# Four graph layers on one core: the features enter in rows, three split steps are kept from pass 3 to pass 4, and the timetables of the layer norm work change

## What is computed

```
x = ln(x + L0(x));  L0: h = relu(adj @ (f1 * (adj @ (x @ W1)))),  out = adj @ (f2 * (adj @ (h @ W2)))
x = ln(x + L1(x));  L1: concat(x, adj @ x) @ Wcat
x = ln(x + L2(x));  L2: m = x @ W_msg + b;  g = sigmoid((m@W_q)(m@W_k).T / sqrt(128) + bias) * adj * adj
                        r = relu(concat(x, g @ m) @ W_upd + b_upd);  out = ln(r) * gamma + beta
x = ln(x + L3(x));  L3: twice: x = swish((adj @ x) @ W3 + b3)
```

## Time and profile before

| | us |
|---|---|
| median of 3 runs | 1653.19 (1652.88 to 1653.26) |
| the profiled execution | 1654.23 |
| its span | 1652.4 |

### The profile page before, as it was taken

The page is one execution under the profiler, slowest core; times in us unless marked ns, Lnnn a source line. Parts: engine busy times, 40 slices in busy tenths (PEclk is TensorE's granted clock), DMA queues, the critical chain, the costliest instruction groups (busy, mean ns, idle before and its releaser), DMA issues.

```text
span 1652.4 us, 19276 instructions
## 1 busy us (share of the span) xinstructions
PE 1605.6 (97%) x7674; PEld 766.8 (46%) x7674; DVE 1212.3 (73%) x1181; ACT 1099.3 (67%) x784; POOL 56.0 (3%) x49
## 2 busy tenths in 40 slices
PE   7999999999999999999999899999999999999997
PEld 4444444444444444444554444444354444444443
DVE  5867547754675568666998698998989986553886
ACT  5767648756778567855666587796878685453753
POOL 2000000000000000000000000100000100000011
PEclk9999999999999999999999999999999999999999
DMA  9988798979699889986888345554545898764983
GB/s 360 416 315 354 283 427 337 369 284 427 269 417 427 333 314 372 411 321 263 355 309 305 140 180 180 178 209 172 199 163 199 312 375 303 282 235 173 351 295 118
DMA packets 67562, 484.56 MB, mean 293 GB/s; under 512 B 7712, under 2 KB 7872, under 8 KB 9232
## 3 DMA queue, kind: packets, MB, share of 16 engines
q1 hardware_dynamic: 66240, 478.70, 75.2%
q0 software_dynamic: 1088, 4.56, 0.8%
q10 hardware_dynamic: 144, 0.07, 0.0%
HBM read 414.09 MB, written 69.21 MB: 292 GB/s over the span
## 4 chain that ended last, share of the span: by engine, by line
PE 81%; DVE 10%; issue 5%; ACT 3%; DMA 1%; POOL 0%; SPq 0%; DVEq 0%; POOLq 0%; ACTq 0%
PE acc L594 34%; PE acc L606 17%; PE spare L594 12%; PE spare L606 6%; PE spare L629 4%; PE rows L498 3%; DVE a_lo L998 3%; DVE a_lo L989 3%; PE acc L629 2%; PE rows L491 1%; DVE bn L905 1%; ACT a_hi L792 1%; DMA a_ring<-adj_dram 1%; DVE gates L1011 1%; ACT gates L822 1%
## 5 line engine op out<-in xcount | busy, mean ns | idle before, releaser
L989 DVE SCALAR_TENSOR_TENSOR a_lo<-a_ring,a_hi 128x2048 f16<-128x2048 f32 x320 | 723.9, 2287 | 321.9 <-ACT a_hi L792 316.5
L792 ACT ACTIVATE a_hi<-a_ring 128x2048 f16<-128x2048 f32 x320 | 604.9, 1905 | 286.7 <-PE spare L594 156.1
L594 PE MATMUL acc<-a_hi,y_hi 128*128 128x512 f16 x1536 | 459.9, 380 | 4.2 <-ACT a_hi L792 3.5
L594 PE MATMUL acc<-a_hi,y_lo 128*128 128x512 f16 x1536 | 459.5, 380 | 0.0
L606 PE MATMUL acc<-a_lo,y_hi 128*128 128x512 f16 x1536 | 406.2, 380 | 9.1 <-DVE a_lo L998 4.9
L606 PEld LDWEIGHTS acc<-a_lo,y_hi 128*128 128x128 f16 x1536 | 149.7, 98 | 193.5 <-DVE a_lo L998 8.1
L594 PEld LDWEIGHTS acc<-a_hi,y_lo 128*128 128x128 f16 x1536 | 150.7, 98 | 182.3 <-issue 2.2
L594 PEld LDWEIGHTS acc<-a_hi,y_hi 128*128 128x128 f16 x1536 | 150.5, 98 | 182.0 <-issue 6.0
L1011 DVE SCALAR_TENSOR_TENSOR gates<-gates,a_ring 128x1024 f32<-128x1024 f32 x128 | 155.8, 1218 | 35.8 <-ACT gates L822 35.6
L805 ACT ACTIVATE a_hi<-gates 128x1024 f16<-128x1024 f32 x128 | 134.8, 1053 | 41.2 <-DVE gates L1011 41.0
L998 DVE TENSOR_TENSOR a_lo<-gates,a_hi 128x1024 f16<-128x1024 f32 x128 | 155.5, 1215 | 0.0
(11 more groups left out here) (119 smaller groups left out, 760.9 us busy)
## 6 DMA issues: line engine op xcount, KB each, us to landing
a_ring<-adj_dram SPq DMA_DIRECT2D x326, 1024.0 KB, 7.4
saved_squares<-squares SPq DMA_DIRECT2D x64, 1024.0 KB, 12.6
a_ring<-saved_squares SPq DMA_DIRECT2D x64, 1024.0 KB, 4.8
x_T<-xt_dram SPq DMA_DIRECT2D x4, 512.0 KB, 8.6
x_rows<-x_dram POOLq DMA_DIRECT2D x1, 2048.0 KB, 12.9
out_dram<-x_rows POOLq DMA_DIRECT2D x3, 512.0 KB, 2.9
out_dram<-x_rows SPq DMA_DIRECT2D x2, 256.0 KB, 2.0
w<-W_dram POOLq DMA_DIRECT2D x2, 64.0 KB, 5.4
```

Source lines behind the costliest of these rows:

```text
L594: mm = pe.matmul(sums[:, h * BANK:(h + 1) * BANK], blk(y[:, y_pass % 2, :], st.j0 + s), slot(a_hi, st)[:, s, h * BANK:(h + 1) * BANK], sta ...
L792: act.activation(slot(a_hi, st), loaded(st), ACT.Copy, scale=2.0 ** A_EXP).then_inc(s_ahi, 1)
L989: dve.scalar_tensor_tensor(out=slot(a_lo, st).rearrange("p s c -> p (s c)"), in0=loaded(st).rearrange("p s c -> p (s c)"), scalar=2.0 ** A ...
```

## The change

- Pass 0 has no projection any more. SP loads `x` in rows in the place of the transposed input, ACT and DVE split it as it is, and the epilogue of pass 1 multiplies by W1 where it transposed (adj @ (x @ W1) = (adj @ x) @ W1). POOL's load of `x` goes.
- `KEPT` has an entry for pass 3: three steps of its first block stay for pass 4, in the room of `x_T`, and of `xn` and `tmp`. `lead` and `halves_free` follow.
- The squares of (0,2) move from pass 2 to pass 4, those of (1,1) from 4 to 2.
- The fifth pass's last chunk, whose epilogue lies in the gated pass, gets a table of its own (`LAST_FIFTH`): evacuation at 1, statistics in two pieces at 4 and 5, normalising at 7, and the rest up to 17.
- In the gated pass the first layer norm is applied by ACT in four pieces of two blocks (`normalise_first`, `xn` = the normalised value), gamma and the residual are two half-size operations each on DVE, statistics come in pieces, the second normalising is four pieces at 26 to 29, y_high is at 30 and y_low at 31 (both at 23 before). The last chunk's table moves one stage later.
- ACT makes one sigmoid of a single column after y_high of chunk 2 of pass 5, which puts the load of the sigmoid's table there.
- In the tail the second half's moments come ahead of the first half's normalising.

```diff
-SAVED_IN = {(2, 0): 1, (3, 0): 1, (3, 1): 1, (2, 3): 2, (1, 3): 2, (0, 3): 2, (0, 2): 2, (1, 0): 3, (2, 1): 3,
-            (3, 2): 3, (1, 2): 4, (0, 1): 4, (3, 3): 3, (2, 2): 3, (1, 1): 4, (0, 0): 4}
+SAVED_IN = {(2, 0): 1, (3, 0): 1, (3, 1): 1, (2, 3): 2, (1, 3): 2, (0, 3): 2, (0, 2): 4, (1, 0): 3, (2, 1): 3,
+            (3, 2): 3, (1, 2): 4, (0, 1): 4, (3, 3): 3, (2, 2): 3, (1, 1): 2, (0, 0): 4}
...
-KEPT = [(i, (j * GROUP + t) * SJ) for i, j, t in ((0, 0, 3), (0, 3, 0), (0, 2, 2), (0, 2, 3), (1, 3, 1), (1, 3, 2))]
+def kept_steps(*steps):
+    return [(i, (j * GROUP + t) * SJ) for i, j, t in steps]
+
+
+IN_SQUARES, IN_X_T, IN_ROWS = RING, RING + SQUARE_SLOTS, RING + SQUARE_SLOTS + 2
+KEPT = {3: dict(zip(kept_steps((1, 1, 1), (1, 1, 2), (1, 1, 3)), (IN_X_T + 1, IN_ROWS, IN_X_T))),
+        7: dict(zip(kept_steps((0, 0, 3), (0, 3, 0), (0, 2, 2), (0, 2, 3), (1, 3, 1), (1, 3, 2)),
+                    (IN_SQUARES, IN_SQUARES + 1, IN_SQUARES + 2, IN_SQUARES + 3, IN_X_T, IN_X_T + 1)))}
...
+SECOND_USES = [n for n, u in enumerate(UNITS) if u.p != u.step.p]
...
-LENGTH = {0: 1, 1: 4, 2: 3, 3: 4, 4: 8, 5: 11, 6: 23, 7: 4, 8: 10, LAST_GATED: 14}
+LAST_GATED, LAST_FIFTH = 10 + GATED, 15
+LENGTH = {0: 1, 1: 4, 2: 3, 3: 4, 4: 8, 5: 11, 6: 32, 7: 4, 8: 10, LAST_GATED: 15, LAST_FIFTH: 17}
 
 
 def timing(p, k):
 
-    return LAST_GATED if (p, k) == (GATED, NC - 1) else p
+    return {(GATED, NC - 1): LAST_GATED, (5, NC - 1): LAST_FIFTH}.get((p, k), p)
...
         def lead(st):
 
             n = LAST_IN_PASS[st.n - RING] + 1 if st.n >= RING else 0
-            return max(n, FIRST_USE[st.n] - RING) if st.p == PASSES else n
+            return max(n, FIRST_USE[st.n] - RING) if any(n <= u < FIRST_USE[st.n] for u in SECOND_USES) else n
 
         def halves_free(eng, st, used):
 
             n = SLOT[st.n]
             if HALVES_BEFORE[st.n] is not None:
                 eng.wait_ge(used, freed(st))
-            elif n >= RING + SQUARE_SLOTS:
+            elif n >= IN_ROWS:
+                eng.wait_ge(s_wqk_product, 1)
+                eng.wait_ge(s_bias, 2 * BIAS_STEPS)
+            elif n >= IN_X_T and st.p > GATED:
                 eng.wait_ge(s_rows, nth("rows", GATED, NC - 1))
-            elif n >= RING:
+            elif IN_SQUARES <= n < IN_X_T and st.p > GATED:
                 eng.wait_ge(s_lg, NB * NC)
+            elif IN_SQUARES <= n < IN_X_T:
+                for t in range(SQUARE_SLOTS):
+                    eng.wait_ge(s_stored[t], 16 * len(SQUARED) // SQUARE_SLOTS)
...
-            if n < RING + SQUARE_SLOTS:
-                v = squares[:, n - RING, :].bitcast(F16)
+            if n < IN_X_T:
+                c = n - IN_SQUARES
+                pair = squares[:, 0:SJ, :] if t is a_hi else squares[:, SJ:2 * SJ, :]
+                return pair.bitcast(F16)[:, :, c * CH:(c + 1) * CH]
+            if n == IN_ROWS:
+                v, at = (xn_T if t is a_hi else tmp_T).bitcast(F16), 0
             else:
-                v = x_T[:, (n - RING - SQUARE_SLOTS) * SJ * CH:(n - RING - SQUARE_SLOTS + 1) * SJ * CH].bitcast(F16)
-            at = 0 if t is a_hi else SJ * CH
+                v = x_T[:, (n - IN_X_T) * SJ * CH:(n - IN_X_T + 1) * SJ * CH].bitcast(F16)
+                at = 0 if t is a_hi else SJ * CH
...
-                sp.dma_start(x_T[:, ic * CH:(ic + 1) * CH], xt[:, ic * CH:(ic + 1) * CH]).then_inc(s_xt[ic], 16)
+                sp.dma_start(x_chunk(0, ic), x[:, ic * CB:(ic + 1) * CB, :]).then_inc(s_x[ic], 16)
...
-                if p in (1, 3, 4):
+                if p in (3, 4):
                     transposes(lambda b: blk(z_T, b))
                 elif p == 5:
                     by_node((x_T_chunk(p, k), wcat[:, 0, :]), (z_T, wcat[:, 1, :]))
                 elif p == 6:
                     bias(bupd_rows)
                     by_node((x_T_chunk(p, k), wupd[:, 0, :]), (z_T, wupd[:, 1, :]), begins=False)
-                elif p == 0:
-                    by_node((x_T_chunk(p, k), w1[:, :]))
+                elif p == 1:
+                    by_node((z_T, w1[:, :]))
...
-                0: {0: [project]},
...
-                LAST_GATED: {1: [project]},
+                LAST_GATED: {2: [project]},
+                LAST_FIFTH: {2: [project], 9: [x_transposes], 11: [messages], 13: [queries], 16: [message_rows]},
...
+                if p == 0:
+                    act.wait_ge(s_x[k], 16)
...
+            def sigmoid_table(p, k):
+
+                if k == 2:
+                    act.activation(stats[:, 2, 0:1], gbias[:, 0:1], ACT.Sigmoid)
...
+            def normalise_first(blocks):
+                def go(p, k):
+                    act.wait_ge(s_shift, 2 * k + 1)
+                    for b in blocks:
+                        op = act.activation(xn[:, b, :], val[:, b, :], ACT.Identity, bias=stats[:, 2, b:b + 1],
+                                            scale=stats[:, 1, b:b + 1])
+                    if blocks[-1] % HB == HB - 1:
+                        op.then_inc(s_first, 1)
+                return go
...
-                    9: [qk_high(1, qT_hi, Q_EXP)], 10: [y_high]},
-                6: {1: [evacuate], 5: [relu], 20: [normalise_again(range(HB))], 21: [normalise_again(range(HB, CB))],
-                    23: [y_high]},
+                    9: [qk_high(1, qT_hi, Q_EXP)], 10: [y_high, sigmoid_table]},
+                6: {1: [evacuate], 5: [relu], 13: [normalise_first([0, 1])], 14: [normalise_first([2, 3])],
+                    15: [normalise_first([4, 5])], 16: [normalise_first([6, 7])], 26: [normalise_again([0, 1])],
+                    27: [normalise_again([2, 3])], 28: [normalise_again([4, 5])], 29: [normalise_again([6, 7])],
+                    30: [y_high]},
                 7: {0: [evacuate], 2: [silu], 3: [y_high]},
                 8: {0: [evacuate], 3: [silu]},
-                LAST_GATED: {0: [evacuate], 3: [relu], 11: [normalise_again(range(CB))], 14: [y_high]},
+                LAST_GATED: {0: [evacuate], 4: [relu], 12: [normalise_again(range(CB))], 15: [y_high]},
+                LAST_FIFTH: {1: [evacuate], 10: [save_x_T], 12: [save_m_T], 13: [qk_high(0, kT_hi, K_EXP)],
+                    14: [qk_high(1, qT_hi, Q_EXP)], 17: [y_high]},
...
+            def some_stats(ready, stage, blocks):
+                def go(p, k):
+                    dve.wait_ge(ready, nth(stage, p, k))
+                    block_stats(blocks)
+                return go
+
+            def all_stats(run):
+                def go(p, k):
+                    join_stats(range(CB), CB * (nth("root", p, k, run) - 1))
+                return go
+
+            def gamma_half(h):
+                def go(p, k):
+                    dve.wait_ge(s_first, HALVES * k + h + 1)
+                    dve.tensor_tensor(half(xn, h), half(xn, h), gam[:, :].unsqueeze(1).to_broadcast([P, HB, F]),
+                                      ALU.mult).then_inc(s_scaled, 1)
+                return go
+
+            def residual_half(h):
...
+                    dve.wait_ge(s_xb, k + 1)
+                    dve.wait_ge(s_scaled, HALVES * k + h + 1)
+                    op = dve.tensor_tensor(half(val, h), half(xn, h), half(x_chunk(p, k), h), ALU.add)
+                    if h == HALVES - 1:
+                        op.then_inc(s_res, 1)
+                return go
...
-                6: {8: [ln_moments(0, s_nl, "nonlin")], 10: [times_gamma], 13: [affine_residual],
-                    16: [ln_moments(1, s_res, "resid")], 19: [shift], 23: [y_low]},
+                6: {6: [some_stats(s_nl, "nonlin", [0, 1])], 7: [some_stats(s_nl, "nonlin", [2, 3])],
+                    8: [some_stats(s_nl, "nonlin", [4, 5])], 9: [some_stats(s_nl, "nonlin", [6, 7]), all_stats(0)],
+                    11: [shift(0)], 16: [gamma_half(0)], 17: [residual_half(0)], 18: [gamma_half(1)],
+                    19: [residual_half(1)], 20: [some_stats(s_res, "resid", [0, 1, 2, 3])],
+                    21: [some_stats(s_res, "resid", [4, 5, 6, 7])], 22: [all_stats(1)], 24: [shift(1)], 31: [y_low]},
                 7: {3: [y_low]},
                 8: {0: [take_over], 5: [residual], 6: [ln_moments(0, s_res, "resid")], 7: [normalise]},
-                LAST_GATED: {4: [ln_moments(0, s_nl, "nonlin")], 5: [times_gamma], 6: [affine_residual],
-                    8: [ln_moments(1, s_res, "resid")], 10: [shift], 14: [y_low]},
+                LAST_GATED: {5: [ln_moments(0, s_nl, "nonlin")], 6: [times_gamma], 7: [affine_residual],
+                    9: [ln_moments(1, s_res, "resid")], 11: [shift(1)], 15: [y_low]},
+                LAST_FIFTH: {3: [values], 4: [some_stats(s_val, "val", [0, 1, 2, 3])],
+                    5: [some_stats(s_val, "val", [4, 5, 6, 7]), all_stats(0)], 7: [normalise],
+                    14: [qk_low(0, kT_hi, kT_lo, K_EXP)], 15: [qk_low(1, qT_hi, qT_lo, Q_EXP)], 17: [y_low, add_beta]},
...
             moments_half(0)
+            moments_half(1)
             normalise_half(0)
-            moments_half(1)
             normalise_half(1)
...
```

(14 more changed lines are left out.)

57 lines of the change are left out of this document (28 added, 29 removed).

## The result

The changed kernel takes 1641.16 us (median of 4 runs, 1640.63 to 1642.51) against 1653.22 (1652.88 to 1655.44) for the kernel before on the same chip: ratio 0.9925, 95% interval 0.9911 to 0.994. That is 12.1 us less, where 16.5 was forecast. It is faster, by 0.7%, and inside the range of 1628 to 1645. It is outside the 1632.5 to 1640.5 that the forecast called its own, by 0.7 us, and close to the 1641.5 to 1641.9 of the rivals (b), (c) and (e).

The account below looks back on a forecast made before the run. PE's pace, 2.59 us per step of 12 products, bounds the kernel outside waits, start and tail; -8.8 + 3.4 - 1.9 + 0.8 - 5.9 - 9.1 + 6.1 - 1.1 = -16.5 us gives 1636.7, range 1628 to 1645.

Parts of the forecast that it names:

- (b): At the start: the DMA holds it, 4.8 us less gained, time 1641.5; chance 0.12.
- (c): Gated chunks: waits stay in another form, gain only 1.3 us per chunk, 3.9 in all, time 1641.9; chance 0.12.
- (e): Start and pass 7: three more half-clock stretches of 3.4 us, +5.1, time 1641.8; chance 0.06.
- Part 5: Entry to pass 7: longer chain to y_low +4.4, half clock behind PE's wait +1.7, together +6.1 us (0 to +7).
- Part 2: Steps kept from pass 3 to 4: -1.9 us (0 to -2.5); squares moved to pass 2: +0.8 (0 to +3).
- Part 4: Gated chunks: waits go, -11.7 us; ACT's pieces cost +2.6 at two chunk ends; together -9.1 (-5 to -11.7).
- The start's 1.2 for a DMA without lead: First ten steps: 1.2 us taken off the 10.0 gain, as PE needs 405 GB/s against the DMA's 421.
- (a): Pass 7 doesn't begin later, as ACT and DVE leave the gated pass further ahead: 6.1 less, 1630.6; chance 0.14.
- (d): Gated pass: ACT becomes the bound through its pieces, gated chunks +14.4 us, time 1660.2; chance 0.04.

Follow-up runs that it names:

- The old pieces: The changed kernel with the epilogue of the gated pass's first three chunks as before the change (24 stages, statistics in one piece): 1646.91 us, 5.8 more.

## Why the prediction was right, and where its sizes were off

Sign, order of size and the named places held, but for the chunks, 89.05 us apart where 87 to 89 was named. The gain was 12.1 of a forecast 16.5, and outside the forecast's own range. The parts, from the first product's start of the same unit in the two profiles:

| part | forecast | profiles | undone or done alone |
|---|---|---|---|
| x in rows, W1 in pass 1 | -5.4 | -4.7 | -3.1 alone |
| kept steps; squares moved | -1.9; +0.8 | -2.2; +0.8 | -2.8 (kept) |
| pass 5, units 284 to 300 | none | +0.7 | in four of 13 profiles |
| entry to the gated pass, from unit 300 | -5.9 | -6.3 | -4.8 |
| gated chunks | -9.1 | -8.1 | -5.8 |
| entry to pass 7 | +6.1 | +7.1 | +2.8 |
| tail | -1.1 | -0.8 | -2.4, with a half clock |
| half clock in pass 4 | none | +1.7 | in one of this kernel's two profiles |
| sum | -16.5 | -11.8 | |

**Right as worked out.** The tenth step at 38.95 for 39.2, because DVE is last: from 22.75 on its a_lo and y_lo follow one another without a pause, 2.2 and 1.1 us each. The squares cost 0.8 and no more. The entry to the gated pass lost both waits and the half clock, 6.3 us in ten of the eleven profiles that have the new table, and 6.4 in the one without the early load. The entry to pass 7 took 4.4 us more before its clock is counted, the very sum of one a_lo 2.2, y_lo 1.2 and ACT 1.0. (The stretch of the earlier trace rows is not quite "without a pause": DVE waits 2.85 us for a_hi at 1326.83 before, and as long at 1313.13 after, so the difference stands.) The old pieces bear this split out: there the 2.2 of y_lo and ACT are absent, and from the gated pass's end to block (0,3) that kernel loses 2.2 where the changed one loses 4.4.

**The step that failed: the clock.** Part 5 spoke of "less left half clock behind it" and priced it at 1.7 us, one stretch of 3.4 as in the earlier trace rows. It was 6.8 us long in both profiles of the changed kernel, and in three of the six others with the same wait of 4.6; it was 3.4 in the other three. 1.3 us of it lay in the wait itself, the other 5.5 cost half, 2.7. Nothing at all was set down for pass 4, where the a_lo wait of 2.1 had run at full clock in the profile before. Part 2 said that the later waits of passes 4 and 5 have nothing changed ahead of them, and that is so for the waits. What follows a wait is another matter. Together these are 2.7 of the 4.7 us that the profiles fall short.

**The other mis-sized terms.** Part 4 gave 1.3 us to a chunk's end, 4 x 0.25 + 0.3; the 89.05 less PE's own 86.9 and the 0.4 leaves 1.8. The cost per step with pieces was even smaller than put (2.72 less 2.59, 0.13 against 0.25, which was 0.3 a few lines earlier), but ACT does not come to them on time: it starts 1.1 late, since its a_hi wait for DVE's gates, and with nothing to absorb it in the single buffer, the whole 1.7 is PE's. The start's 1.2 for a DMA without lead was 1.7 in the first profile, and from 1.1 to 3.0 over all of them. The tail's DVE work ends 1.1 sooner behind the last product, as forecast (7.1 against 8.2), but only 0.8 reaches the end of the span. The 0.7 in pass 5 was not foreseen: the chain to DVE's normalise of chunk 0 begins there at a load that landed at 790.35, while in a profile without the loss PE is not held by a load.

**The rivals.** (a) and (d) are excluded: pass 7 does begin later, and ACT is no bound. (b) is partly alive: the start's lead varies by 1.9 us between profiles, and the part alone gave 3.1. (c) fell: the old waits went, 8.1 us in the profiles. By the time alone (b), at 1641.5, came closest, but the start lost 0.5 us to its forecast and not 4.8. (e), at 1641.8, has the right reason, half clock in pass 7, and one place it did not name. That three rivals lie within 1 us of the result, and the forecast 4.5 from it, shows how little the time alone tells.

**Not additive.** By the single edits the parts sum to -3.1 - 2.8 - 4.8 - 5.8 + 2.8, and -1.1 for the tail, -14.8, against -12.1; with the 0.8 of the squares, which have no run of their own, -14.0. Some of it is spread between runs. One overlap is shown: of the gated pass's 7.9 us, 2.2 only bring PE sooner to a y_lo that comes no sooner. What a wait's end is worth downstream has to be read at the next place with a fixed chain.

## What to carry to other kernels

Follow a gain to the next chain that it doesn't shorten: the pieces that freed DVE inside the chunks put y_lo and y_hi of chunk 2 into the chain to pass 7, and moving those again, with a table set back and one step of pass 4 moved, was worth 8.5 us beside the change's 12.1. When work is cut into pieces for another engine, ask not only what a piece adds per step but how late that engine already is on arrival, and where the first place without a second buffer comes. A wait of 2 us on PE should be priced with a chance of half clock behind it, here 7 in 23 (next section), and its removal with the same.
